# Mamba block with a mixture of experts: one state of each group from its own product, and two adds done by DMAs

## The chip, the cores and the metric

The kernel runs on one core of a Trainium2 chip. The metric is the device time of one execution in microseconds. A core has a matrix engine (TensorE, PE in the profile), a vector engine (DVE), a scalar engine (ACT), a general engine (POOL) and a synchronising engine (SP) that issues transfers here. Each runs its own list of instructions in order, and they wait for each other on semaphores.

## The reference

x is 8 sequences of 1024 tokens by 256 channels. It goes through a layer norm, a Mamba block and a residual add, then a layer norm, a mixture of experts and another residual add:

```
xp, z = in_proj(layernorm(x))                 # 2 x 512 channels
xc    = silu(causal_conv4(xp))
dt, B, C = x_proj(xc)                         # 64, 16, 16 columns
delta = softplus(dt_proj(dt) + dt_b)
h_n[t] = exp(delta * A_n) * h_n[t-1] + delta * xc * B_n[t]     # 16 states n for each of 512 channels
y     = sum_n h_n * C_n + D * xc
x     = x + out_proj(y * silu(z))
x     = x + square(relu(xn @ Ws1)) @ Ws2 + routed experts      # xn = layernorm(x)
```

The weights of the routed experts are cut to whole numbers, so a routed part is added only where a weight reaches 1. A flag decides at the end whether that path runs.

## The kernel before

The tokens are worked in NQ = 16 chunks of CH = 512 tokens. Channels are split into G = 4 groups of 128 partitions, and the 16 states of a group are worked in pairs. So a chunk has S = 32 steps (s = 0 to 31), eight for each group; step s of group g handles states 2(s % 8) and 2(s % 8) + 1. k = 32c + s counts steps over all chunks. Each engine's program is one hand-written loop over c and s; what an engine does in step s stands there as `if s == ...` (`tensor` L446, `scalar` L805, `vector` L1116, `gpsimd` L1326, `sync` L1435). A number such as ("yt", -1, 3) in the tables below means: group 3 of stage yt, of the chunk before.

The core of a step:
- ACT computes the decay factors da = exp(delta * A_n), five steps ahead (`act_exp`, L624, a pair for each step).
- PE computes BX, the input term of four states at once (`pe_bx`, L225): 16 products of 32 x 128 by 32 x 128, from uT (u = delta * xc, transposed) and bd (B spread on diagonals). BX takes four PSUM banks and exists once, so a fill for states 4p to 4p + 3 waits until the four scans of the fill before it are done. Fills stand at the end of odd steps.
- DVE runs one scan for each state (`dve_scan`, L964), from da and BX to hs.
- POOL multiplies hs by C (`pool_times_c`, L1261), and PE sums it into Y by transposing products (`pe_sum`, L257, for step k - 2).

Around it, in fixed steps, stands all other work of neighbouring chunks: the projections and convolution of chunks ahead (`pe_z`, `pe_xp`, `pe_dbc`, `pe_dt`, `pe_ut`; `dve_tap` is one tap of the convolution, `dve_delta` and `act_softplus` make delta), the gate and output projection of the chunk before (`dve_gate`, `pe_yt`, `pe_out`, stage "res"), and its experts (`pe_hidden`, `pe_htr`, `pe_shared`, stage "o"). `dve_residual` (L1068) adds x to "res" and `dve_shared` (L1109) adds "o", both in x1, which SP had loaded with x (`sp_xr`, L1418) and later writes out (`sp_out`, L1430).

Eight PSUM banks exist: four for BX, two for Y (shared with the convolution), and PA and PB for everything else. The tables BANK_A and BANK_B (L17, L20) give the order in which stages use PA and PB, by step. `bank_uses` numbers the uses; a PE product for use n waits until use n - 1 has been read out and released (`e.wait_ge(out, n)`), and the reader releases it by `.then_inc(out, 1)`. Which engine releases a stage is in the code of the reader: `act_z`, `act_yt`, `act_ut`, `act_trc` on ACT, `dve_delta`, `dve_residual`, `dve_shared`, `dve_top` on DVE.

The lines that order ACT around two of these releases:

```
if s == 16:                                   # L873
    act_softplus(e, c, 3)
...
if s == 30 and on(c + 1):                     # L901
    act_softplus(e, c + 1, 1)
    act_z(e, c + 1, 2)
```

## Time and profile before

| | us |
|---|---|
| median of 3 runs | 1560.38 |
| lowest, highest | 1560.03, 1560.77 |
| span of the profiled execution | 1559.1 |
| busy PE, DVE, POOL, ACT in the span | 1454.6, 1475.8, 1399.0, 1257.4 |

The profiled execution spans 1559.1 us from its first to its last instruction, 1.3 us below the median of the runs. The first scan starts at 34.5 us and the last ends at 1537, with 16 chunks between them. TensorE's granted clock is 0.999 of full speed. A profile's timeline has one line for each run of like instructions: start, duration, engine, source line, operation, output <- inputs, shapes and number of records; in brackets how long the engine was idle just before and who ended that.

### The profile page before, as it was taken

How to read it: one execution, taken by the hardware profiler on the slowest of the kernel's cores; microseconds unless marked ns; L12 is line 12 of the kernel's file. 1: busy time of each engine (PE TensorE's matmuls, PEld its weight loads, DVE VectorE, ACT ScalarE, POOL GpSimd, SP SyncE). 2: the span in 40 equal slices, each digit the busy share in tenths (PEclk: the TensorE clock that was granted, in tenths of full speed). 3: DMA queues.
4: the chain of work that ended last, by engine and by line, in shares of the span. 5: the costliest groups of instructions: out<-in, count | busy, mean ns of one | idle time of the engine just before them, and what ended most of it. 6: DMA issues, size and time to landing. Idle time of an engine off the chain costs nothing.

```text
span 1559.1 us, 39641 instructions
## 1 busy us (share of the span) xinstructions
PE 1454.6 (93%) x15324; PEld 1134.1 (73%) x15324; DVE 1475.8 (95%) x1775; ACT 1257.4 (81%) x2099; POOL 1399.0 (90%) x1199
## 2 busy tenths in 40 slices
PE   8889999999999999999999999999999999999988
PEld 5666777776777777777777777767777677777777
DVE  6999999999999999999999999999999999998886
ACT  7987887887888888887887888888888887788752
POOL 2899999999999999998999989999998999989994
PEclk9999999999999999999999999999999999999999
DMA  5103031040402305032040301304031040401301
GB/s 161 61 3 136 2 101 66 9 157 3 143 22 65 101 3 164 1 93 73 4 163 3 138 28 47 120 3 164 2 97 69 4 149 3 137 15 43 123 2 56
DMA packets 78512, 106.48 MB, mean 68 GB/s; under 512 B 42289, under 2 KB 67761, under 8 KB 70130
## 3 DMA queue, kind: packets, MB, share of 16 engines
q1 hardware_dynamic: 78322, 103.92, 20.8%
q8 instruction: 123, 2.02, 0.5%
q14 instruction: 67, 0.55, 0.1%
HBM read 86.10 MB, written 17.30 MB: 66 GB/s over the span
## 4 chain that ended last, share of the span: by engine, by line
DVE 32%; PE 20%; ACT 18%; issue 17%; POOL 10%; DMA 1%; SPq 1%; DVEq 1%; ACTq 0%; POOLq 0%
DVE hs L974 29%; PE BX L239 9%; ACT da L638 8%; POOL hs L1271 8%; PE Y L299 3%; PE Y L263 2%; ACT xc L705 1%; DMA cb<-c_scratch 1%; SPq L1406 1%; ACT xp L673 1%; DVE st L986 1%; DVE Y L1005 1%; PE PB L349 1%; ACT x2n L775 1%; POOL rstd L1304 1%
## 5 line engine op out<-in xcount | busy, mean ns | idle before, releaser
L1271 POOL TENSOR_TENSOR hs<-hs,cb 128x1024 f32<-128x1024 f32 x512 | 1210.2, 2364 | 76.3 <-DVE hs L974 55.3
L974 DVE TENSOR_TENSOR_SCAN hs<-da,BX 128x512 f32<-128x512 f32 x1024 | 1165.6, 1201 | 55.5 <-PE BX L239 46.5
L638 ACT ACTIVATE da<-delta,a_neg 128x511 f32<-128x511 f32 (+1 forms) x1024 | 663.6, 711 | 24.9 <-DVE hs L974 24.5
L263 PEld LDWEIGHTS Y<-ident,hs 128*128 128x128 f32 x4096 | 464.5, 141 | 97.3 <-issue 58.0
L263 PE MATMUL Y<-ident,hs 128*128 128x128 f32 x4096 | 510.1, 273 | 14.5 <-POOL hs L1271 14.4
L239 PE MATMUL BX<-bd,uT 32*128 32x128 f32 x8192 | 301.3, 284 | 77.9 <-DVE hs L974 73.8
L239 PEld LDWEIGHTS BX<-bd,uT 32*128 32x128 f32 x8192 | 252.5, 187 | 138.8 <-DVE hs L974 137.7
L299 PE MATMUL Y<-xnT,w_in 128*128 128x512 f32 x240 | 117.6, 613 | 0.7 <-ACT gate L691 0.7
L673 ACT ACTIVATE xp<-Y 128x512 f32<-128x512 f32 x60 | 35.9, 598 | 100.4 <-PE Y L299 99.9
L324 PE MATMUL PA<-w_in,xnT 128*128 128x512 f32 x240 | 114.5, 599 | 0.0
L1005 DVE SCALAR_TENSOR_TENSOR Y<-xp,w_conv,Y 128x512 f32<-128x512 f32 x120 | 88.9, 741 | 3.0 <-ACT Y L675 1.4
L1289 POOL TENSOR_TENSOR u<-delta,xc 128x512 f32<-128x512 f32 x63 | 80.4, 1277 | 5.1 <-issue 5.1
L1267 POOL COPY hlast<-hs 128x2 f32<-128x2 f32 x256 | 47.7, 186 | 38.5 <-DVE hs L974 36.8
L324 PEld LDWEIGHTS PA<-w_in,xnT 128*128 128x128 f32 x240 | 43.2, 190 | 44.9 <-issue 43.1
L741 ACT ACTIVATE u<-PB 128x512 f32<-128x512 f32 x63 | 37.5, 596 | 46.8 <-PE PB L349 45.1
L349 PE MATMUL PB<-dbc,w_dt 97*128 97x512 f32 x126 | 70.9, 645 | 0.9 <-DVE dbc L1136 0.9
L758 ACT ACTIVATE uT<-PB 128x512 f32<-128x512 f32 x48 | 28.7, 597 | 49.8 <-PE PB L357 49.8
L299 PEld LDWEIGHTS Y<-xnT,w_in 128*128 128x128 f32 x240 | 40.8, 190 | 36.5 <-issue 28.7
L333 PE MATMUL PA<-xc,w_x 128*96 128x512 f32 x128 | 61.6, 603 | 0.2 <-ACT xc L687 0.2
L376 PE MATMUL PB<-w_out,ygT 128*128 128x256 f32 x240 | 60.8, 386 | 0.9
L376 PE MATMUL PA<-w_out,ygT 128*128 128x256 f32 x240 | 60.8, 386 | 0.0
L1281 POOL TENSOR_TENSOR da<-first,hlast 128x2 f32<-128x2 f32 x256 | 51.1, 199 | 0.0
(194 smaller groups left out, 1517.5 us busy)
## 6 DMA issues: line engine op xcount, KB each, us to landing
cb<-c_scratch SPq DMA_DIRECT2D x64, 1024.0 KB, 4.8
x<-in_x SPq DMA_DIRECT2D x16, 512.0 KB, 4.3
x_scratch<-x2T SPq DMA_DIRECT2D x16, 512.0 KB, 6.8
xt<-in_x SPq DMA_DIRECT2D x15, 512.0 KB, 5.3
bd<-bt SPq DMA_DIRECT2D x480, 1.0 KB
out<-x SPq DMA_DIRECT2D x15, 512.0 KB, 3.2
w_in<-in_in_wT SPq DMA_DIRECT2D x1, 1024.0 KB, 8.4
c_scratch<-dbc SPq DMA_DIRECT2D x64, 8.0 KB, 1.5
```

The costliest lines, as they stand in the source:

```text
L239: mm = e.matmul(BX[:, q * CH + j * P:q * CH + (j + 1) * P], uT[rows, g, j, :], bd[rows, (NR * c + p) % BR, j, :, :].rearrange("p t n -> p ...
L263: mm = e.matmul(Y[(G * c + g) % 2][:, t * P:(t + 1) * P], hs[:, k % HR, q, t * P:(t + 1) * P], ident[:, :], is_transpose=True, start=False ...
L299: mm = e.matmul(bank[:, :], w_in[:, kk, g * P:(g + 1) * P], xnT[c % 2][:, kk, :], start=(kk == 0), stop=(kk == KD - 1))
L324: mm = e.matmul(bank[:, :], xnT[c % 2][:, kk, t * P:(t + 1) * P], w_in[:, kk, ED:2 * ED], start=(kk == 0), stop=(kk == KD - 1))
L333: mm = e.matmul(PA[0:FX, :], w_x[:, g, :], xc[:, (G * c + g) % XR, :], start=(g == 0), stop=(g == G - 1))
L349: e.matmul(bank[:, :], w_dt[:, g * P:(g + 1) * P], dbc[:, :].rearrange("f (j q t) -> f q j t", j=J, q=RT), start=True, stop=True).then_inc ...
L376: mm = e.matmul(bank[:, t2 * DM:(t2 + 1) * DM], ygT[:, g, t * P:(t + 1) * P], w_out[:, g, :], start=(g == 0), stop=(g == G - 1))
L638: e.activation(da[:, k % DR, q, h:], delta[:, g, h:], ACT.Exp, scale=a_neg[:, g, n:n + 1]).then_inc(s_da, 1)
L974: e.tensor_tensor_scan(hs[:, k % HR, q, :], da[:, k % DR, q, :], BX[:, :].rearrange("p (t n) -> p n t", n=RT)[:, n % RT, :], float(c % HV) ...
L1005: e.scalar_tensor_tensor(out=bank[:, :], in0=xp[:, g, kk:kk + CH], scalar=w_conv[:, g, kk:kk + 1], in1=bank[:, :], op0=ALU.mult, op1=ALU.a ...
L1271: e.tensor_tensor(hs[:, k % HR, :, :], hs[:, k % HR, :, :], cb[:, Q * p:Q * p + Q, :], ALU.mult).then_inc(s_hc, 1)
L1289: e.tensor_tensor(u[:, m % UR, :].rearrange("p (j q t) -> p q j t", j=J, q=RT), delta[:, g, :].rearrange("p (q j t) -> p q j t", j=J, q=RT ...
```

## The change

1. The last state of each group (15) no longer comes from BX. `pe_bu` computes its input term for 512 tokens by four products of uT (128 x 128) and b_diag, in which `act_diag` lays the 16th column of B on the diagonal (four small ACT operations a chunk). It is written to PA or PB at steps 7, 15, 23 and 31. The scan of that state reads that bank, and the refill of BX waits for 15 scans of a group instead of 16, so that it can run beside the 16th. The last BX fill of a group has 96 columns instead of 128 in each product.
2. `dve_residual` and `dve_shared` are gone. ACT copies "res" from its bank to x1, and "o" to x2n (`act_res`, `act_shared`). POOL issues a DMA that adds x from memory to x1 (`pool_add_x`, step 15), and one that adds x2n to the output in memory (`pool_add_shared`, step 3); SP writes x1 out at step 20 of the next chunk and loads no x into x1.
3. The orders are changed to fit: the bank tables, and the steps of several PE, ACT, DVE and POOL operations. bt has two buffers, and prob shares is_top's memory.

The diff, cut to its core:

```diff
@@ -14,12 +14,14 @@
 EXPS = "natural_log_exp_and_others"
 
 
-BANK_A = {0: [("z", 0, 3)], 2: [("o", -2, 1)], 4: [("yt", -1, 3)], 7: [("z", 1, 0)], 10: [("ut", 0, 2)], 11: [("res", -1, 1)],
-          12: [("trc0", 2, 0)], 16: [("z", 1, 1)], 18: [("dbc", 1, 0)], 22: [("bt", 1, 0)],
-          24: [("otr", -1, 0)], 25: [("otr", -1, 1)], 27: [("hl", -1, 1)], 30: [("z", 1, 2)]}
-BANK_B = {0: [("o", -2, 0)], 2: [("ut", 0, 1), ("trc", 2, 0)], 3: [("trc", 2, 1)], 4: [("yt", -1, 2)], 6: [("dt", 0, 2)],
-          8: [("res", -1, 0)], 13: [("trc0", 2, 1)], 15: [("yt", 0, 0)], 16: [("dt", 0, 3)], 20: [("ut", 0, 3)], 21: [("yt", 0, 1)], 24: [("dt", 1, 0)],
-          26: [("hl", -1, 0)], 28: [("ut", 1, 0)], 29: [("ht", -1, 0)], 30: [("dt", 1, 1), ("yt9", 0, 2)]}
+BANK_A = {0: [("z", 0, 3)], 1: [("o", -2, 0)], 2: [("dt", 0, 2)], 4: [("yt", -1, 3)], 6: [("trc", 2, 1)], 7: [("bu", 0, 0)],
+          10: [("ut", 0, 2)], 11: [("res", -1, 1)], 12: [("trc0", 2, 0)], 16: [("z", 1, 1)], 18: [("dbc", 1, 0)],
+          22: [("bt", 1, 0)], 23: [("bu", 0, 2)], 24: [("otr", -1, 0)], 25: [("otr", -1, 1)], 27: [("hl", -1, 1)],
+          30: [("z", 1, 2)], 31: [("bu", 0, 3)]}
+BANK_B = {2: [("o", -2, 1)], 3: [("yt", -1, 2)], 4: [("ut", 0, 1)], 5: [("trc", 2, 0)], 6: [("z", 1, 0)],
+          8: [("res", -1, 0)], 13: [("trc0", 2, 1)], 14: [("yt", 0, 0)], 15: [("bu", 0, 1)], 16: [("dt", 0, 3)],
+          20: [("ut", 0, 3)], 21: [("yt", 0, 1)], 24: [("dt", 1, 0)], 26: [("hl", -1, 0)], 28: [("ut", 1, 0)],
+          29: [("ht", -1, 0)], 30: [("dt", 1, 1), ("yt9", 0, 2)]}
 
...
@@ -225,7 +235,7 @@
         def pe_bx(e, m):
             c, i = divmod(m, QC)
             g, p = divmod(i, NR)
-            e.wait_ge(s_scan, RT * m)
+            e.wait_ge(s_scan, (N - 1) * (m // NR) + RT * p)
             if p == 0:
                 _, n, _, out = bank_of("ut", c, g)
                 e.wait_ge(out, n + 1)
@@ -233,13 +243,24 @@
                 e.wait_ge(s_bd, p + 1)
             if g == 0 and c:
                 e.wait_ge(s_bdd, 16 * KT * c)
+            ns = RT - 1 if p == NR - 1 else RT
             for j in range(J):
                 for q in range(RT):
                     rows = slice(q * KT, (q + 1) * KT)
-                    mm = e.matmul(BX[:, q * CH + j * P:q * CH + (j + 1) * P], uT[rows, g, j, :],
-                                  bd[rows, (NR * c + p) % BR, j, :, :].rearrange("p t n -> p (t n)"), start=True,
+                    mm = e.matmul(BX[:, q * CH + j * P:q * CH + (j + 1) * P].rearrange("p (t n) -> p t n", n=RT)[:, :, 0:ns],
+                                  uT[rows, g, j, :], bd[rows, (NR * c + p) % BR, j, :, 0:ns], start=True,
                                   stop=True, tile_position=(q * KT, 0))
             mm.then_inc(s_bx, 1)
+
+        def pe_bu(e, c, g):
+            bank, n, done, out = bank_of("bu", c, g)
+            e.wait_ge(out, n)
+            e.wait_ge(s_bdiag, c + 1)
+            e.wait_ge(*released("ut", c, g))
+            for j in range(J):
+                mm = e.matmul(bank[:, :].rearrange("p (q j t) -> p j q t", q=RT, j=J)[:, j, :, :], uT[:, g, j, :], b_diag[:, j, :],
+                              start=True, stop=True)
+            mm.then_inc(done, 1)
 
         def pe_skip(e, c, g):
             m = G * c + g
...
-                    if s == 2:
-                        pe_ut(e, c, 1)
-                    if s == 6:
-                        pe_dt(e, c, 2)
...
@@ -499,15 +516,16 @@
                         pe_xp(e, G * c + s // NP + 6)
                     if s == 0 and c:
                         pe_z(e, c, 3)
-                    if s in (0, 2) and on(c - 2):
-                        pe_shared(e, c - 2, s // 2)
-                    if s == 2 and c and on(c + 2):
-                        pe_trc(e, c + 2, 0)
+                    if s in (1, 2) and on(c - 2):
+                        pe_shared(e, c - 2, s - 1)
+                    if s == 2:
+                        pe_dt(e, c, 2)
                     if s in (12, 13) and c == 0:
                         pe_trc(e, 2, s - 12)
                     if on(c - 1):
+                        if s == 3:
+                            pe_yt(e, c - 1, 2)
                         if s == 4:
-                            pe_yt(e, c - 1, 2)
                             pe_yt(e, c - 1, 3)
...
+                    if s == 4:
+                        pe_ut(e, c, 1)
                     if on(c + 1):
-                        if s == 7:
+                        if s == 6:
                             pe_z(e, c + 1, 0)
...
@@ -532,6 +552,8 @@
                             pe_bt(e, c + 1)
                     if s == 24 and on(c + 1):
                         pe_dt(e, c + 1, 0)
+                    if s % NP == NP - 1:
+                        pe_bu(e, c, s // NP)
...
@@ -539,13 +561,13 @@
                     if s == 29 and on(c - 1):
                         pe_htr(e, c - 1)
                     if s == 30 and on(c + 1):
+                        pe_z(e, c + 1, 2)
                         pe_dt(e, c + 1, 1)
-                        pe_z(e, c + 1, 2)
                     if k >= 2:
                         pe_sum(e, k - 2)
-                    if s == 3 and c and on(c + 2):
-                        pe_trc(e, c + 2, 1)
-                    if s == 15:
+                    if s in (5, 6) and c and on(c + 2):
+                        pe_trc(e, c + 2, s - 5)
+                    if s == 14:
                         pe_yt(e, c, 0)
...
+        def act_diag(e, c):
+            if c:
+                e.wait_ge(*released("bt", c, 0))
+                e.wait_ge(*written("bu", c - 1, G - 1))
+            else:
+                e.wait_ge(s_b15, 1)
+                e.wait_ge(s_ident, 1)
+            for j in range(J):
+                ins = e.activation(b_diag[:, j, :], ident[:, :], ACT.Copy, scale=bt[c % 2][:, NR - 1, j, RT - 1:RT])
+            ins.then_inc(s_bdiag, 1)
...
+        def act_res(e, c, kk):
+            bank, n, done, out = bank_of("res", c, kk)
+            e.wait_ge(done, n + 1)
+            e.wait_ge(s_out, 16 * c)
+            e.activation(x1[:, 2 * kk:2 * kk + 2, :], bank[:, :].rearrange("p (t d) -> p t d", t=2), ACT.Copy).then_inc(out, 1)
+
+        def act_shared(e, c, kk):
+            bank, n, done, out = bank_of("o", c, kk)
+            e.wait_ge(done, n + 1)
+            e.activation(x2n[:, 2 * kk:2 * kk + 2, :], bank[:, :].rearrange("p (t d) -> p t d", t=2), ACT.Copy).then_inc(out, 1)
+
         def act_norm2(e, c):
             e.wait_ge(*shifted2(c))
-            for kk in range(2):
-                e.wait_ge(*released("res", c, kk))
-            if on(c - 1):
-                for kk in range(2):
-                    e.wait_ge(*written("o", c - 1, kk))
+            e.wait_ge(s_res, 16 * (c + 1))
+            e.wait_ge(s_acc, 16 * c)
             for t in range(TB):
                 ins = e.activation(x2n[:, t, :], x1[:, t, :], ACT.Identity, bias=shift2[:, t:t + 1],
                                    scale=rstd2[:, t:t + 1])
...
                         act_exp(e, 4)
                     if s == 1 and c:
                         act_z(e, c, 3)
+                    if s in (2, 3) and on(c - 2):
+                        act_shared(e, c - 2, s - 2)
                     if s == 2:
-                        act_ut(e, c, 1)
-                    if s in (3, 4) and c and on(c + 2):
-                        act_trc(e, c + 2, s - 3)
+                        act_softplus(e, c, 2)
+                    if s == 3 and on(c - 1):
+                        act_yt(e, c - 1, 2)
+                    if s in (5, 6) and c and on(c + 2):
+                        act_trc(e, c + 2, s - 5)
                     if s == 4 and c and on(c + 1):
                         act_xp(e, G * c + 6)
                     if s == 4 and on(c - 1):
-                        act_yt(e, c - 1, 2)
                         act_yt(e, c - 1, 3)
-                    if s == 6:
-                        act_softplus(e, c, 2)
+                    if s == 4:
+                        act_ut(e, c, 1)
                     if s == 10:
                         act_ut(e, c, 2)
+                    if s in (11, 15) and on(c - 1):
+                        act_res(e, c - 1, s // 4 - 2)
...
@@ -907,19 +955,22 @@
                         act_exp(e, k + DR - 1)
                     if s == 0 and c:
                         act_skip(e, c, 0)
-                    if s == 8:
-                        act_silu_z(e, c)
+                    if s == 5:
+                        act_diag(e, c)
                     if s in (12, 13) and c == 0:
                         act_trc(e, 2, s - 12)
                     if s == 7:
                         if on(c + 1):
                             act_z(e, c + 1, 0)
                         act_skip(e, c, 1)
+                    if s == 8:
+                        act_silu_z(e, c)
                     if s == 5 and c == 0:
                         act_norm(e, 2)
+                    if s == 14:
+                        act_yt(e, c, 0)
                     if s == 15:
                         act_skip(e, c, 2)
-                        act_yt(e, c, 0)
...
-        def dve_scan(e, k):
+        def dve_scan(e, k, q):
             c, i = divmod(k, S)
             g, p = divmod(i, NP)
-            e.wait_ge(s_bx, k // 2 + 1)
-            e.wait_ge(s_y, max(0, k - HR + 1))
-            if c % HV:
-                e.wait_ge(s_cr, S * (c // HV) + i + 1)
-            for q in range(Q):
-                n = Q * p + q
-                e.wait_ge(s_da, Q * k + q + 1)
+            if q == 0:
+                e.wait_ge(s_bx, k // 2 + 1)
+                e.wait_ge(s_y, max(0, k - HR + 1))
+                if c % HV:
+                    e.wait_ge(s_cr, S * (c // HV) + i + 1)
+            n = Q * p + q
+            e.wait_ge(s_da, Q * k + q + 1)
+            if n == N - 1:
+                bank, use, done, out = bank_of("bu", c, g)
+                e.wait_ge(done, use + 1)
+                e.tensor_tensor_scan(hs[:, k % HR, q, :], da[:, k % DR, q, :], bank[:, :],
+                                     float(c % HV), ALU.mult, ALU.add).then_inc(out, 1)
+            else:
                 e.tensor_tensor_scan(hs[:, k % HR, q, :], da[:, k % DR, q, :],
                                      BX[:, :].rearrange("p (t n) -> p n t", n=RT)[:, n % RT, :],
                                      float(c % HV), ALU.mult, ALU.add).then_inc(s_scan, 1)
...
+                    if s == 13 and on(c + 1):
+                        dve_tap(e, G * c + 7 if c else G + 3, 0)
+                        dve_tap(e, G * c + 7 if c else G + 3, 1)
+                    if s == 14 and on(c + 1):
+                        dve_tap(e, G * c + 7 if c else G + 3, 2)
...
+                    if s == 24 and on(c + 2):
+                        dve_tap(e, G * c + 8, 0)
+                    if s == 25:
+                        if on(c + 2):
+                            dve_tap(e, G * c + 8, 1)
+                        if on(c + 1):
+                            dve_delta(e, c + 1, 0)
+                        if on(c + 2):
+                            dve_tap(e, G * c + 8, 2)
...
+                    if s == 28 and on(c - 1):
+                        dve_top(e, c - 1, 1)
+                    if s == 29 and on(c + 2):
+                        dve_tap(e, G * c + 9, 0)
+                        dve_tap(e, G * c + 9, 1)
...
+        def pool_add_x(e, c):
+            for kk in range(2):
+                e.wait_ge(*released("res", c, kk))
+            e.dma_start(x1[:, :, :], x_v[c], accum_op=ALU.add).then_inc(s_res, 16)
+
+        def pool_add_shared(e, c):
+            for kk in range(2):
+                e.wait_ge(*released("o", c, kk))
+            e.wait_ge(s_out, 16 * (c + 1))
+            e.dma_start(out_v[c], x2n[:, :, :], accum_op=ALU.add).then_inc(s_acc, 16)
...
-                        if s == 7:
+                        if s == 1 and c:
+                            pool_u(e, c, 1)
+                        if s == 4:
                             pool_u(e, c, 2)
                         if s == 17:
                             pool_u(e, c, 3)
-                    if on(c + 1):
-                        if s == 25:
-                            pool_u(e, c + 1, 0)
-                        if s == 31:
-                            pool_u(e, c + 1, 1)
+                    if s == 3 and on(c - 2):
+                        pool_add_shared(e, c - 2)
+                    if s == 15 and on(c - 1):
+                        pool_add_x(e, c - 1)
+                    if s == 25 and on(c + 1):
+                        pool_u(e, c + 1, 0)
```

SP's `sp_x` moves from step 6 to 8, and `pe_fill`, which keeps PE busy in the last two chunks, stands in one step less. Before the loops, one small DVE copy is added for the first chunk's b_diag.

## Rows read from the trace of the kernel before

**Rows 1.** The page: busy time by engine; scans and their idle time ahead.
```profile
PE 1454.6 (93%) x15324; PEld 1134.1 (73%) x15324; DVE 1475.8 (95%) x1775; ACT 1257.4 (81%) x2099; POOL 1399.0 (90%) x1199
...
L974 DVE TENSOR_TENSOR_SCAN hs<-da,BX 128x512 f32<-128x512 f32 x1024 | 1165.6, 1201 | 55.5 <-PE BX L239 46.5
```
**Rows 2.** Busy time by engine in one chunk (span, PE, PEld, DVE, ACT, POOL).
```profile
786.10:879.99 93.89, 88.87 (x945) 69.09 (x945) 91.51 (x111) 78.27 (x132) 87.30 (x75) 1.00 0.22 72
```
**Rows 3.** Timeline of PE: start, duration (us), line, out<-in, records, idle before.
```profile
797.16 0.60 PE L273 MATMUL PB<-ident,xt 128*128 128x128 f32 x4
...
803.64 1.17 PE L239 MATMUL BX<-bd,uT 32*128 32x128 f32 x32
...
804.75 1.12 PE L349 MATMUL PB<-dbc,w_dt 97*128 97x512 f32 x2
...
805.71 1.04 PE L263 MATMUL Y<-ident,hs 128*128 128x128 f32 x8
...
806.59 1.88 PE L324 MATMUL PA<-w_in,xnT 128*128 128x512 f32 x4
...
809.54 1.17 PE L239 MATMUL BX<-bd,uT 32*128 32x128 f32 x32 [0.20 <-DVE hs L974]
...
828.19 2.00 PE L376 MATMUL PA<-w_out,ygT 128*128 128x256 f32 x8
...
850.53 1.17 PE L239 MATMUL BX<-bd,uT 32*128 32x128 f32 x32 [0.17 <-DVE hs L974]
...
853.46 0.50 PE L340 MATMUL PA<-ident,dbc 96*128 96x96 f32 x4
...
856.38 1.17 PE L239 MATMUL BX<-bd,uT 32*128 32x128 f32 x32 [0.68 <-DVE hs L974]
...
862.44 1.17 PE L239 MATMUL BX<-bd,uT 32*128 32x128 f32 x32
...
864.03 1.09 PE L396 MATMUL PB<-w_hr,x2T 128*128 128x136 f32 x8
```
**Rows 4.** Timeline of DVE, the same columns.
```profile
809.40 0.72 DVE L1009 SCALAR_TENSOR_TENSOR xc<-xp,w_conv,Y 128x512 f32<-128x512 f32 x1
...
810.04 0.68 DVE L1044 SCALAR_TENSOR_TENSOR delta<-PB,u 128x512 f32<-128x512 f32 x1
...
810.78 4.55 DVE L974 TENSOR_TENSOR_SCAN hs<-da,BX 128x512 f32<-128x512 f32 x4
...
821.68 0.68 DVE L1072 TENSOR_TENSOR x<-x,PB 128x512 f32<-128x512 f32 x1
...
874.64 0.24 DVE L1082 MAX8 top<-PA 128x8 f32<-128x8 f32 x2
...
874.91 0.17 DVE L1084 TENSOR_TENSOR is_top<-PA,top 128x16 f32<-128x16 f32 x1
```
**Rows 5.** Timeline of ACT, the same columns.
```profile
797.80 0.60 ACT L654 ACTIVATE xnT<-PB 128x512 f32<-128x512 f32 x1 [0.36 <-PE PB L273]
...
805.91 0.60 ACT L741 ACTIVATE u<-PB 128x512 f32<-128x512 f32 x1
...
807.74 2.55 ACT L638 ACTIVATE da<-delta,a_neg 128x512 f32<-128x512 f32 x4
...
810.19 0.58 ACT L699 ACTIVATE gate<-PA 128x512 f32<-128x512 f32 x1
...
878.23 0.58 ACT L699 ACTIVATE gate<-PA 128x512 f32<-128x512 f32 x1
...
885.30 0.57 ACT L699 ACTIVATE gate<-PA 128x512 f32<-128x512 f32 x1
```
**Rows 6.** The page: POOL's product; loads of x (KB, us to landing); SP's timeline.
```profile
L1271 POOL TENSOR_TENSOR hs<-hs,cb 128x1024 f32<-128x1024 f32 x512 | 1210.2, 2364 | 76.3 <-DVE hs L974 55.3
...
x<-in_x SPq DMA_DIRECT2D x16, 512.0 KB, 4.3
...
801.66 0.38 SPq L1423 DMA_DIRECT2D x<-in_x  x1
```

193 lines of the change are left out of this document (84 added, 109 removed).

## The prediction

> **What bounds the kernel now.** I read the busy times first. The page puts DVE at 95% of the span, PE at 93% and POOL at 90% [rows 1]. The stretch from 786.10 to 879.99 us is one whole chunk (from its first BX fill to the next chunk's): 93.89 us, with DVE 91.51, PE 88.87, POOL 87.30 and ACT 78.27 us busy [rows 2]. Three engines are nearly full, so shares alone don't say what a freed microsecond is worth; the order of work does.
>
> The timelines of PE and DVE show a loop of two steps, which I call a period (16 in a chunk; period p holds steps 2p and 2p+1). PE fills BX (1.10 us), DVE scans its four states (4.55 us), and only then may PE fill again. Next scans start 1.24 us after a fill starts (809.54 to 810.78), so the loop can't be shorter than about 5.85 us, as 850.53 to 856.38 shows (5.90 behind two taps, 803.64 to 809.54) [rows 3, 4]; 16 x 5.85 = 93.6 of the 93.89 us. DVE's other work (two short operations, about 1.35 us) stands in the 1.30 us in which it would wait for the fill; its recorded idle there is 46.5 us in the whole run [rows 1]. PE has 4.75 us in a period for all work that is not the fill, and mostly needs 4.3 to 4.6. So the bound is a loop, and **PE has under half a microsecond to spare in most periods**.
>
> **Prices.** A PE burst's duration contains some 0.17 us of tail that the next burst overlaps (1.04 us, next start 0.87 or 0.88 later). With it taken off: eight transposes of hs 0.87, dt 0.96, a z or xp product 1.72 (1.82 behind a fill), a product of 256 columns in eight records 1.83 behind a fill, a transposed tile of four records 0.43 [rows 3]. pe_bu has no row of its own. It is four float32 products of 128 columns, eight records; the nearest row is eight records of 136 columns, 1.09 less 0.17 = 0.92 us, so 0.87. Bounds: 0.43 (four records) and 1.83 (eight of 256 columns) [rows 3]. On ACT, dt's start to the softplus' start is 1.16 us, its three operations take 1.83 until the next begins, one step's pair of exps 1.23, a copy out of a bank 0.58; PE goes on at once when the copy ends. A transpose of x handed over takes 0.64 + 0.60 = 1.24 us until its bank is free [rows 3, 5].
>
> **What is taken off.** Four adds of 0.68 us a chunk leave DVE [rows 4]. The fourth scan of a group's last period no longer reads BX, so that period could be 5.85 - 1.14 = 4.71 us (a scan is issued every 1.14 us). By DVE alone, with its new order, a chunk is: eight periods of 5.85, two of 5.90 (two taps), three of 4.71 (p3, p11, p15), p7 with a tap between its scans 5.35, p12 7.10, p14 6.35, together 91.45 us.
>
> **DVE's own losses.** Step 24 gets a tap between scans (0.64), and step 25 three operations behind its scans: 4.47 + 0.64 + 1.99 = 7.10 us instead of 6.06 (fills 856.38 to 862.44) [rows 3]. In p14, a max and compare (0.43) now stand between scans, and two taps behind: 6.35 instead of 5.85. The two taps of step 23 were free inside a wait [rows 4].
>
> **PE's work in the group ends.** Each now has pe_bu. p11: 1.10 fill + 1.82 xp + 0.33 bt + 0.87 bu + 1.74 sums = 5.86 us. p3: 1.10 + 1.82 + 0.43 + 0.87 + 1.74 = 5.96. So PE, not the scans, ends these periods, and the 4.71 is not reached: the gain of hiding the refill is gone before any wait is counted. The fill itself shrinks from 128 to 96 columns; bounds 0 and 0.27 us (a quarter), I take 0.15, since shorter products of the same number of records save a little less than in proportion [rows 3].
>
> **The banks.** PE and ACT each run in order, and a product may enter PA or PB only when the use before it is released. Four handovers become waits, each followed from the fill's start F:
> - *p1.* pe_yt of group 2 follows pe_shared(1) in PB. Its release, act_shared(1), is at ACT's step 3, behind softplus(2), which waits for dt(2), issued in the same step 2. dt starts at F + 1.24 + 0.44 (skip) + 0.87 (shared) = 2.55; ACT starts at 3.71, ends the softplus at 5.54, the exps at 6.77, the copy at 7.37; then yt 0.43 and sum 0.87: 8.70 instead of 5.85, **+2.85 us**. Behind this wait on PE are the transposes and the next fill, and DVE waits for that.
> - *p15.* z(2) now goes ahead of dt(1) on PE, but ACT still does softplus(1) before it copies z(2), and pe_bu(3) needs z's bank. dt starts at 2.92, ACT at 4.08, ends softplus at 5.91, z at 6.49; bu and sum 1.74: 8.23 instead of 5.85, less what the shorter fill saves: **+2.3 us**.
> - *p0.* The z(3) copy ended 7.64 us after the z(2) copy began [rows 5], since exps and norm lie between. It now ends at F + 5.32, and pe_shared(0), which moved to step 1 in the same bank, would start at 3.79: 7.10 instead of 5.85, **+1.25 us** in chunks 2 to 13.
> - *p3 and p7.* pe_bu stands directly behind trc(1) or yt(0) in the same bank. The release is 1.24 us after the transposes start, where 0.43 was enough. p3: 3.79 + 1.26 + 0.87 + 0.87 = 6.79; p7: 3.75 + 2.96 = 6.71. Less 0.15: **+0.8 and +0.7 us**.
> p2 gains a transpose: 5.95, +0.1.
>
> **POOL, ACT, DMA.** POOL gets two DMA issues a chunk. No row shows one on this queue; the bounds are 0.38 us (an issue on SP) and 2.36 us (one of POOL's own products), and I take 1 us, nearer the issue [rows 6]. 87.30 + 2 stays below even the 91.45 us of DVE's own work, so it costs nothing. The Trainium skill, page DMA: Bandwidth & Descriptors (Latency and other measured facts), gives about 1 us for the first byte on GpSimd's path against 0.6 us; no row here shows it, and the sum would be the same by it. The load of x lands after 4.3 us [rows 6]; the adding DMA is issued about F8 + 4.2 and needed by stats2 at F8 + 12.2, so 8 us cover it. ACT gains four copies (2.3 us) and four small products (about 0.9), and has 15 us free; nothing beyond the orders above.
>
> **The sum.** Chunks 2 to 13: 2.85 + 2.3 + 1.25 + 0.8 + 0.7 + 0.1 + 1.05 + 0.5 - 0.15 = 9.4 us each, 113 us. Chunk 1 has no shared product (5.3), chunk 0 none and no transposes of x (2.5), chunk 14 no xp (4.7), chunk 15 only p1 and p7 against faster group ends (1.3). Together 127 us on the profiled execution's span of 1559.1; the median stands 1.3 us above the span. 1560.4 + 127 is **1687 us**.
>
> **The rivals.**
> *Faster.* The handovers do not bite, and PE's new products go into gaps. Then DVE's 91.45 us rules: 2.4 us less in each of 15.5 chunks, 1523 us. It needs PE's other work in a group end below 3.6 us; the rows add up to 4.6 to 4.9. It also needs ACT to release shared(1) before dt's softplus, against its order. The skill's page Perfetto Trace Analysis (Identifying the Most-Contended Engine) says that busy time of matmuls is no measure of headroom and weight loads are; those are busy 69 of 93.89 us [rows 2], which by that rule leaves room. In this trace PE's next burst starts where the last ends, whatever the loads show. Chance 5%.
> *Partly absorbed.* The waits overlap more than I add (bu is at its lower bound of 0.43 us in all four group ends, 1.76 us a chunk, and ACT has the z(3) copy done in time, 1.25 us): 6.4 us in each of the twelve chunks and 10 us for the other four, about 1647 us. Chance 14%.
> *The adding DMA is late.* If it takes 11 us instead of 8, stats2 at step 19 stands ahead of DVE's scans and 3 us a chunk come on top: 1687 + 15 x 3 = 1732 us. It decides from 8 us on. For it: adding means a read as well as a write of x1. Against it: SP's loads land in half of that. Chance 10%.
> *No change.* Gain and waits balance: 2%.
> My forecast has 69%, and by itself reaches from 1655 to 1715. The range, 1638 to 1725, takes in the absorbed case and leaves out most of the late DMA. Faster by over 0.2% (about what a measurement can tell here) 5%, within it 2%, slower 93%.
>
> **What would show it.** In the profile after: PE waits of about 3 us on ACT's copy of the shared product ahead of the gate transposes in step 3, and of some 1.7 us on the z copy ahead of pe_bu in step 31; fills 8.7, 8.2 and 6.7 us apart at p1, p15 and p3/p7; DVE's idle ahead of scans up from 46.5 to over 150 us; POOL and ACT with more idle time. The prediction is wrong if fills at the group ends stand 4.7 us apart, if a row of pe_bu's eight records is under 0.5 us, or if DVE's idle ends on the DMA.

## The result, and the profile after

The changed kernel takes **1734.69 us** (median of 4 runs, 1732.35 to 1735.69) against 1560.3 us before: a ratio of 1.1114, 95% interval 1.1098 to 1.113. The forecast was 1687 us with a range of 1638 to 1725. The direction and the places were right, the size was not: the loss is 171.4 us by the two spans (1730.5 less 1559.1) where 127 were predicted.

The page of the changed kernel, in the parts shown of before in [rows 1] (busy time by engine; the scans with their idle time and what ended it; the gate transposes of step 3; the adding DMA of x with its KB and its time to landing):

```profile
span 1730.5 us, 40837 instructions
PE 1537.1 (89%) x15824; PEld 1203.8 (70%) x15824; DVE 1449.5 (84%) x1718; ACT 1309.2 (76%) x2221; POOL 1438.8 (83%) x1228
L1031 DVE TENSOR_TENSOR_SCAN hs<-da,BX 128x512 f32<-128x512 f32 x960 | 1099.2, 1202 | 156.0 <-PE BX L250 153.8
L1028 DVE TENSOR_TENSOR_SCAN hs<-da,PA 128x512 f32<-128x512 f32 x48 | 58.5, 1218 | 75.4 <-ACT da L662 63.4
L386 PE MATMUL PB<-ident,gate 128*128 128x128 f32 x192 | 35.1, 313 | 39.8 <-ACT x2n L811 39.8
x<-in_x POOLq DMA_DIRECT2D x15, 512.0 KB, 5.9
```

No engine is at 90% any more. PE's work grew by 82.5 us, DVE's fell by 26.3, and the scans' idle time went from 55.5 [rows 1] to 156.0 us, plus 75.4 us ahead of the 48 scans of state 15 that read PA. So time is lost in waits. Where, the timeline of PE shows over one chunk (868.84 to 974.61 us, 105.77 against the 93.89 of [rows 2]); these are its steps 0 to 3, 7, 15, and 31:

```profile
868.84 1.17 PE L250 MATMUL BX<-bd,uT 32*128 32x128 f32 x32
...
873.94 1.13 PE L434 MATMUL PA<-w_s,x2n 128*128 128x256 f32 x4 [1.14 <-ACT gate L723]
...
875.87 1.17 PE L250 MATMUL BX<-bd,uT 32*128 32x128 f32 x32
...
879.20 1.04 PE L284 MATMUL Y<-ident,hs 128*128 128x128 f32 x8
883.07 1.12 PE L386 MATMUL PB<-ident,gate 128*128 128x128 f32 x4 [2.84 <-ACT x2n L811]
883.98 1.91 PE L284 MATMUL Y<-ident,hs 128*128 128x128 f32 x8
885.82 1.17 PE L250 MATMUL BX<-bd,uT 32*128 32x128 f32 x32
...
892.00 1.15 PE L250 MATMUL BX<-bd,uT 32*128 32x96 f32 x32
893.08 1.98 PE L345 MATMUL PB<-w_in,xnT 128*128 128x512 f32 x4
...
897.06 1.16 PE L261 MATMUL PA<-b_diag,uT 128*128 128x128 f32 x8 [0.69 <-ACT xnT L678]
898.06 1.04 PE L284 MATMUL Y<-ident,hs 128*128 128x128 f32 x8
899.02 1.17 PE L250 MATMUL BX<-bd,uT 32*128 32x128 f32 x32
...
921.64 1.16 PE L261 MATMUL PB<-b_diag,uT 128*128 128x128 f32 x8 [0.69 <-ACT ygT L800]
...
972.65 1.16 PE L261 MATMUL PA<-b_diag,uT 128*128 128x128 f32 x8 [1.62 <-ACT gate L723]
```

The four handovers are there, with waits of 1.14 us (period 0), 2.84 (1), 0.69 (3 and 7, one handover in the prediction) and 1.62 (15). What the prediction did not have is what comes after the longest: the four transposes and the eight sums, which it priced at 0.43 and 0.87 us until the next starts, take 0.91 (883.07 to 883.98) and 1.84 (to 885.82). The windows of one microsecond around them (columns: length, busy time of PE, PEld, DVE, ACT, POOL, then PE's granted clock, DMA share and GB/s) say why:

```profile
882.00:883.00 1.00, 0.00 (x0) 0.00 (x0) 0.84 (x2) 1.00 (x2) 0.92 (x3) 0.73 0.00 0
883.00:884.00 1.00, 0.93 (x5) 0.93 (x6) 0.00 (x0) 0.02 (x1) 1.00 (x1) 0.50 0.00 0
884.00:885.00 1.00, 1.00 (x6) 1.00 (x5) 0.00 (x0) 0.78 (x2) 1.00 (x2) 0.50 0.07 16
885.00:886.00 1.00, 1.00 (x9) 0.67 (x11) 0.00 (x0) 1.00 (x2) 0.98 (x1) 0.56 0.00 0
886.00:887.00 1.00, 1.00 (x33) 0.88 (x33) 0.00 (x0) 0.04 (x1) 0.00 (x0) 1.00 0.43 32
```

Toward the end of the idle stretch (880.23 to 883.07) the granted clock falls to 0.50, the lower level of 1.2 GHz, and comes back some 3 us later. Fill to fill, the periods of this chunk against the forecast (the other six stayed at 5.85):

| period | 0 | 1 | 2 | 3 | 7 | 11 | 12 | 13 | 14 | 15 |
|---|---|---|---|---|---|---|---|---|---|---|
| before | 5.85 | 5.85 | 5.85 | 5.90 | 5.90 | 5.85 | 6.06 | 5.85 | 5.85 | 5.85 |
| forecast | 7.10 | 8.70 | 5.95 | 6.64 | 6.56 | 5.71 | 7.10 | 5.85 | 6.35 | 8.1 |
| after | 7.03 | 9.95 | 6.18 | 7.02 | 7.03 | 5.97 | 6.60 | 6.26 | 6.24 | 8.38 |

### The profile page after: what moved, and what is told of

Its sections match the earlier page's. It is cut to its first block, busy times and chain, and to the rows that moved or that the text cites. A ratio compares the mean times of both kernels' runs of the same rounds, so it can differ in the third digit from the quotient of the medians.

```text
span 1730.5 us, 40837 instructions
## 1 busy us (share of the span) xinstructions
PE 1537.1 (89%) x15824; PEld 1203.8 (70%) x15824; DVE 1449.5 (84%) x1718; ACT 1309.2 (76%) x2221; POOL 1438.8 (83%) x1228
## 4 chain that ended last, share of the span: by engine, by line
PE 41%; DVE 23%; ACT 18%; issue 12%; POOL 4%; DMA 1%; DVEq 0%; SPq 0%; POOLq 0%; ACTq 0%
DVE hs L1031 20%; PE BX L250 12%; PE Y L284 8%; ACT da L662 7%; PE Y L320 3%; POOL hs L1320 3%; PE PA L345 2%; PE PA L261 2%; PE PA L397 2%; PE PB L345 2%; ACT u L778 1%; ACT xt L668 1%; ACT u L776 1%; PE PB L370 1%; PE PB L386 1%
## 5 line engine op out<-in xcount | busy, mean ns | idle before, releaser
L1031 DVE TENSOR_TENSOR_SCAN hs<-da,BX 128x512 f32<-128x512 f32 x960 | 1099.2, 1202 | 156.0 <-PE BX L250 153.8
L662 ACT ACTIVATE da<-delta,a_neg 128x511 f32<-128x511 f32 (+1 forms) x1024 | 666.0, 712 | 5.5 <-DVE hs L1031 4.9
L284 PEld LDWEIGHTS Y<-ident,hs 128*128 128x128 f32 x4096 | 477.1, 143 | 111.5 <-issue 63.1
L284 PE MATMUL Y<-ident,hs 128*128 128x128 f32 x4096 | 535.0, 277 | 18.9 <-POOL hs L1320 18.6
L1028 DVE TENSOR_TENSOR_SCAN hs<-da,PA 128x512 f32<-128x512 f32 x48 | 58.5, 1218 | 75.4 <-ACT da L662 63.4
L345 PE MATMUL PA<-w_in,xnT 128*128 128x512 f32 x180 | 87.7, 609 | 0.0
L261 PE MATMUL PA<-b_diag,uT 128*128 128x128 f32 x384 | 53.7, 283 | 33.2 <-ACT gate L723 24.3
L1330 POOL TENSOR_TENSOR da<-first,hlast 128x2 f32<-128x2 f32 x256 | 74.7, 292 | 0.0
L261 PEld LDWEIGHTS PA<-b_diag,uT 128*128 128x128 f32 x384 | 46.5, 191 | 40.1 <-ACT gate L723 27.9
L386 PE MATMUL PB<-ident,gate 128*128 128x128 f32 x192 | 35.1, 313 | 39.8 <-ACT x2n L811 39.8
L800 ACT ACTIVATE ygT<-PB 128x512 f32<-128x512 f32 x48 | 28.4, 591 | 54.4 <-PE PB L386 54.4
```

Source lines behind the costliest of these rows:

```text
L261: mm = e.matmul(bank[:, :].rearrange("p (q j t) -> p j q t", q=RT, j=J)[:, j, :, :], uT[:, g, j, :], b_diag[:, j, :], start=True, stop=True)
L284: mm = e.matmul(Y[(G * c + g) % 2][:, t * P:(t + 1) * P], hs[:, k % HR, q, t * P:(t + 1) * P], ident[:, :], is_transpose=True, start=False ...
L345: mm = e.matmul(bank[:, :], xnT[c % 2][:, kk, t * P:(t + 1) * P], w_in[:, kk, ED:2 * ED], start=(kk == 0), stop=(kk == KD - 1))
L662: e.activation(da[:, k % DR, q, h:], delta[:, g, h:], ACT.Exp, scale=a_neg[:, g, n:n + 1]).then_inc(s_da, 1)
L1031: e.tensor_tensor_scan(hs[:, k % HR, q, :], da[:, k % DR, q, :], BX[:, :].rearrange("p (t n) -> p n t", n=RT)[:, n % RT, :], float(c % HV) ...
L1330: e.tensor_tensor(da[:, k % DR, :, 0], first[:, g, Q * p:Q * p + Q], hlast[:, g, Q * p:Q * p + Q], ALU.mult).then_inc(s_cr, 1)
```

## The experiments

Each run is told by its edit, to the changed kernel unless said otherwise. Theory A is in each case the chain of orders as the prediction has it, with what the trace of after added.

**1. ScalarE copies the shared product ahead of the softplus.** The costliest wait, period 1, is laid to the place of one copy in ScalarE's order.

```diff
-                    if s in (2, 3) and on(c - 2):
-                        act_shared(e, c - 2, s - 2)
+                    if s == 2 and on(c - 2):
+                        act_shared(e, c - 2, 0)
+                        act_shared(e, c - 2, 1)
                     if s == 2:
                         act_softplus(e, c, 2)
```

> The changed kernel with one edit: ScalarE copies the second half of the shared product (step 2) ahead of the softplus of group 2 instead of behind it. Theory A (the wait of 2.84 us in period 1 is the place in ScalarE's order, and the half clock is its consequence): the copy ends some 0.1 us before dt(2), so period 1 goes from 9.95 to about 5.9 us, 4.05 us in each of 14 chunks: 57 us less, 1678 us, and the granted clock stays at 1.00 there. Theory B (the half clock has another cause and stays): only the 2.84 us of the wait go, 40 us less, 1695 us. Theory C (the time comes back in another wait, such as uT behind the gate transposes): under 15 us less.

Measured: **1678.75 us**, ratio 1.0763 (1.0745 to 1.0781). Period 1 is 5.85 us in every chunk, the transposes of gate stand right behind the sum, the mean clock is 0.998. From PE's timeline of this run:

```profile
855.35 1.04 PE L284 MATMUL Y<-ident,hs 128*128 128x128 f32 x8
856.22 0.60 PE L386 MATMUL PB<-ident,gate 128*128 128x128 f32 x4
856.66 1.04 PE L284 MATMUL Y<-ident,hs 128*128 128x128 f32 x8
```

`act_shared(0)` stood ahead of the softplus before too, so what moved is the second copy: one copy put ahead of the softplus and the exps behind it is worth 56 us, a third of the loss, as theory A had it to within 1 us. The rival in which only the 2.84 us go (1695) and the one in which the time comes back elsewhere fall. This run shows that wait and clock go together, not yet that the idle time causes the clock.

**2. The wait stays, but TensorE is kept busy in it.** A tile of zeros is transposed and added into Y, 24 times, so nothing in the results or in the order of the others changes.

```diff
                         if s == 3:
+                            if on(c - 2):
+                                pe_zero(e, c, 24)
                             pe_yt(e, c - 1, 2)
```

> The changed kernel with nothing moved; 24 transposes of a tile of zeros, added into Y (which leaves it as it is), stand on TensorE just ahead of the gate transposes of step 3, where it otherwise idles 2.84 us. They take 24 x 0.109 = 2.6 us. Theory A (TensorE's clock falls to its lower level because it idled): the granted clock stays 1.00, the four gate transposes take 0.43 and the eight of hs 0.87 until the next starts, period 1 goes from 9.95 to 8.66; 1.29 us in 13 chunks, 17 us less, 1718 us. Theory B (the slow stretch comes from something else, such as the bank being read by ScalarE or the DMAs of that moment): no gain or a small loss, 1735 us or up to 5 us more.

Measured: **1716.97 us**, ratio 1.0998 (1.098 to 1.1017), period 1 between 8.66 and 8.68 in all 14 chunks from 2 on, mean clock 0.997. PE's timeline of this run (20 of the 24 zero transposes have a record):

```profile
875.25 2.35 PE L296 MATMUL Y<-ident,zt 128*128 128x128 f32 x20
877.83 0.66 PE L396 MATMUL PB<-ident,gate 128*128 128x128 f32 x4 [0.23 <-ACT x2n L823]
878.32 1.04 PE L287 MATMUL Y<-ident,hs 128*128 128x128 f32 x8
879.28 1.17 PE L253 MATMUL BX<-bd,uT 32*128 32x128 f32 x32
```

The transposes of gate take 0.49 and the sums 0.96, so the lower clock had cost 1.30 us of the 2.75. ScalarE's reads and the DMAs are there as before, so those rivals fall: the 17.7 us are the idle engine's lower clock, by themselves. 8.66 us is also what the prediction's sum for period 1 gave (8.70). The clock still falls once in chunks 7 and 13 of the profiled execution, in period 13, where nothing was filled (7.81 and 7.71 us against 6.36 in the other odd chunks).

**3. A third of the filling.** Eight transposes of zeros instead of 24, which leaves 1.97 us idle.

> As the run with 24 transposes of zeros ahead of the gate transposes, but with 8 of them (0.87 us): TensorE still idles some 1.97 us there. Theory A (the idle of 2.84 us is at the edge: the one of 2.55 us in the run with z(2) first kept its clock, and so did that of 2.84 us in chunk 2): the clock is kept, period 1 is 8.66 us, 1717 us, as with 24. Theory B (the wait must be filled for the most part): the clock falls all the same, and the time is that of the changed kernel, 1735 us.

Measured: **1731.96 us**, ratio 1.1093 (1.1075 to 1.1112). Theory A is wrong: only chunks 4, 8 and 10 keep the clock (periods 1 and 2 together 14.85 us). The nine other chunks from 2 to 13 and the last two lose it, at a point that shifts from chunk to chunk, in some so late that it is mostly the fill and the products of period 2 that are hit; in each of the nine the two periods take 16.40 to 16.46 us together. PE's timeline and windows in chunk 9 of this run:

```profile
990.10 0.66 PE L396 MATMUL PB<-ident,gate 128*128 128x128 f32 x4 [1.97 <-ACT x2n L823]
990.60 1.30 PE L287 MATMUL Y<-ident,hs 128*128 128x128 f32 x8
991.82 2.09 PE L253 MATMUL BX<-bd,uT 32*128 32x128 f32 x32
```
```profile
990.00:991.00 1.00, 0.90 (x8) 0.90 (x9) 0.00 (x0) 0.25 (x2) 1.00 (x1) 1.00 0.00 0
991.00:992.00 1.00, 1.00 (x10) 0.67 (x10) 0.00 (x0) 1.00 (x3) 1.00 (x2) 0.61 0.00 0
992.00:993.00 1.00, 1.00 (x20) 1.00 (x24) 0.00 (x0) 0.81 (x2) 0.93 (x2) 0.50 0.00 0
```

Here PE has worked for 1.1 us again when its clock falls. So the length of the one idle stretch doesn't decide it: in the changed kernel 2.84 us kept the clock in chunk 2 (its period 1 is 8.66) and lost it in all later ones, and here 1.97 us lost it in nine chunks of twelve. The 2.55 us of run 4, of which the expectation says that they kept the clock, lost it in chunks 2, 6, 7 and 11. Theory B's 1735 us is near what was measured, but it too had every chunk alike. The Trainium skill, page TensorE: Matmul & The Clock Gate (Part 1: The HAM clock gate), says that the chip's observation of the engine runs freely and is not started by the kernel; that agrees with code that is the same in each chunk and is hit in some. What the runs show is the price: 1.3 to 1.6 us each time it falls in period 1.

**4. ScalarE copies z(2) first.** TensorE writes z(2) ahead of dt(1) since the change, while ScalarE still did softplus(1) first.

```diff
                     if s == 30 and on(c + 1):
-                        act_softplus(e, c + 1, 1)
                         act_z(e, c + 1, 2)
+                        act_softplus(e, c + 1, 1)
```

> The changed kernel with one edit: ScalarE copies z(2) ahead of the softplus of group 1 (step 30), as TensorE now writes it first. Theory A (ScalarE's chain from dt(1) through exps, norm, exps, skip to the z(3) copy runs on its own clock): the wait of 1.62 us ahead of pe_bu goes and period 15 falls from 8.38 to 6.6, but the z(3) copy ends only 0.48 us earlier, so period 0 grows from 7.03 to about 8.3; net 0.5 us in each of 14 chunks, about 1728 us. Theory B (the two waits are independent): 1.8 us in each of 15 chunks, 27 us less, 1708 us.

Measured: **1737.24 us**, ratio 1.1134 (1.1116 to 1.1153), no gain. The wait of 1.62 us ahead of pe_bu is gone and period 15 falls from 8.38 to 6.49, but period 0 rises from 7.03 to 8.44, in four chunks to between 9.75 and 9.94. PE's timeline, period 0:

```profile
872.83 1.04 PE L284 MATMUL Y<-ident,hs 128*128 128x128 f32 x8
876.42 1.13 PE L434 MATMUL PA<-w_s,x2n 128*128 128x256 f32 x4 [2.55 <-ACT gate L723]
```

The wait has moved: the copy of z(3) hangs on ScalarE's chain (softplus, two pairs of exps, a norm of 2 us, exps, skip), and that chain starts with dt(1), not with the fill. A fill that comes 1.9 us earlier waits 1.4 us more there. Two waits that stand in a row behind one chain are one wait. Most of the 9 us above the forecast are the clock again (0.98 on average): the four long periods 0, and 1.6 us instead of 1.3 behind the wait of period 1 in most chunks.

**5. Without pe_bu.** The products of uT and diag(B) and the writes of b_diag are left out, the fill has 128 columns throughout and state 15 is scanned from BX; banks, orders and the adding DMAs stay.

```diff
-                    if s % NP == NP - 1:
-                        pe_bu(e, c, s // NP)
...
-            ns = RT - 1 if p == NR - 1 else RT
+            ns = RT
```

> The changed kernel without its products of uT and diag(B): the fill has 128 columns again, state 15 is scanned from BX, no b_diag is written; all orders, banks and the adding DMAs stay. Theory A (the price of pe_bu is what it adds on TensorE and the handover ahead of it; period 0 and 15 are tied by ScalarE's chain to the z(3) copy): periods 3, 7 and 11 fall from 7.02, 7.03 and 5.97 to 5.85, which is 2.46 us in 15 chunks, 37 us less. Period 15 falls by 2.5 us but period 0 gives it back, and since TensorE then idles some 3.7 us there, its clock falls there too, 1.3 us in 14 chunks: 1716 us (1698 if the clock does not fall). Theory B (pe_bu's wait in period 15 is independent): another 2.5 x 15 us, 1660 us.

Measured: **1747.63 us**, ratio 1.1194 (1.1175 to 1.1213): slower than with the products, and 32 us above theory A. Period 15 is 5.89, and period 0 is 9.55 to 11.33 in chunks 2 to 13. The waits of PE in this run and the windows behind the first of them:

```profile
PE PA L434 <- ACT gate L720: 47.3, 14, 3.7
PE PB L386 <- ACT x2n L808: 39.8, 14, 2.8
PE PB L397 <- ACT gate L720: 12.8, 13, 1.0
```
```profile
882.00:883.00 1.00, 0.00 (x0) 0.00 (x0) 1.00 (x2) 1.00 (x2) 0.92 (x3) 1.00 0.00 0
883.00:884.00 1.00, 0.37 (x1) 0.37 (x2) 0.05 (x1) 1.00 (x3) 1.00 (x1) 0.53 0.53 188
884.00:885.00 1.00, 1.00 (x3) 0.80 (x3) 0.00 (x0) 0.81 (x2) 1.00 (x2) 0.50 0.99 418
```

PE waits 3.7 us in period 0 and its clock falls there too in nine of these twelve chunks (not in 3, 10 and 12); both were expected. What was not: period 4 grows from 5.85 to 6.69, since the residual's product now reaches PB 0.99 us before the z copy has left it (8.38 in the three chunks where the clock falls behind that wait), and period 7 falls only to 6.55, not 5.85, for the third tap now stands between the scans of steps 14 and 15. pe_bu's waits had covered both. So this run doesn't price pe_bu; it shows that what the trace puts ahead of it is in good part owed to orders that were changed with it, and comes up elsewhere when it is gone. Run 8 leaves it out once ScalarE's copies are moved.

**6. Three copies moved.** As 1 and 4 together, and ScalarE copies z(3) at step 0, ahead of a pair of exps, instead of at step 1.

> As the kernel with mended handovers, but with pe_bu back in its place ahead of the sum of hs; only ScalarE's three copies are moved. Theory A (pe_bu behind the sum takes TensorE's wait away and gives it to DVE's scan of state 15 and to GpSimd behind it, so the order is worth little): periods 3 and 7 rise again to 7.02, periods 4, 8 and 10 fall to 5.85, 0.3 to 0.9 us a chunk more: 1640 to 1655 us. Theory B (the order of pe_bu is worth its 1.7 us of waits in full): 1664 us.

Measured: **1645.59 us**, ratio 1.0543 (1.0527 to 1.056), 89 us less than the changed kernel by three copies moved in ScalarE's order, and inside the expected 1640 to 1655. Period 0 is 6.61, period 1 is 5.85, period 15 is 6.49; periods 3 and 7 stand at 7.02 and 7.03.

**7. The sum ahead of pe_bu as well.** This takes away the last two handovers.

```diff
-                    if s % NP == NP - 1:
-                        pe_bu(e, c, s // NP)
...
                     if k >= 2:
                         pe_sum(e, k - 2)
+                    if s % NP == NP - 1:
+                        pe_bu(e, c, s // NP)
```

> The changed kernel with its four handovers mended and nothing else: ScalarE copies both shared products ahead of the softplus of group 2, z(2) ahead of the softplus of group 1, z(3) ahead of the exps of step 0, and TensorE does the sum of hs ahead of pe_bu in steps 7, 15, 23 and 31. Theory A (what is left is TensorE's own work): periods 0 and 1 at 5.85, 2 at 6.18, 3 and 7 at 6.05, 11 at 5.97, 12 to 14 as they are (6.55, 6.31, 6.27), 15 at 6.4 and seven at 5.85, together 96.5 us a chunk against 105.8: 1602 us, still some 2.7% slower than before. Theory B (the handovers were all there was against the change, and its gain appears when they are gone): below 93.9 us a chunk, 1555 us or less.

Measured: **1640.22 us**, ratio 1.0507 (1.0491 to 1.0523). Between the theories and 38 us above A. The forecast of 96.5 us a chunk read only TensorE's bursts; a chunk takes 98.43 or 99.05. Period 3 is 6.14 or 6.55 and not 6.05, 4 is 6.37 or 5.97, 8 is 5.97, 10 is 6.60 in even chunks, period 0 is 6.61. The timelines of DVE and POOL in period 3 of an even chunk, and of PE in its period 10:

```profile
842.04 3.44 DVE L1032 TENSOR_TENSOR_SCAN hs<-da,BX 128x512 f32<-128x512 f32 x3 [0.16 <-PE BX L250]
847.55 1.22 DVE L1029 TENSOR_TENSOR_SCAN hs<-da,PA 128x512 f32<-128x512 f32 x1 [2.07 <-PE PA L261]
...
848.84 0.18 POOL L1317 COPY hlast<-hs 128x2 f32<-128x2 f32 x1 [0.86 <-DVE hs L1029]
...
888.16 1.09 PE L284 MATMUL Y<-ident,hs 128*128 128x128 f32 x8 [0.76 <-POOL hs L1321]
```

pe_bu behind the sum lets PE go on, but DVE's scan of state 15 now waits 2 us for it at each group's end. POOL, which multiplies that state, starts 0.86 us late, and in an even chunk it has little room to make up for it: PE waits for POOL in periods 3 and 10 (0.27, then 0.25 and 0.76 us). Period 7 is 6.16. With run 6 beside it, the order of pe_bu is worth 5.4 us in all and not the 1.7 us a chunk of its waits: most of the wait has only changed its owner.

**8. The same without pe_bu.** The edit of 5 on top of 6.

> As the kernel with mended handovers, but without the products of uT and diag(B): 128 columns in every fill, state 15 scanned from BX. Theory A (pe_bu costs TensorE time in the group ends and hides nothing): periods 3, 7, 11 and 15 at 5.85, or up to 0.7 more where the taps now stand in period 7; 95.5 us a chunk, 1586 us, some 16 us less than with pe_bu. Theory B (the scan of state 15 beside the refill is worth something once nothing waits): slower than with pe_bu.

Measured: **1633.65 us**, ratio 1.0472 (1.0456 to 1.0488). Leaving pe_bu out gains 6.6 us against run 7, less than the 16 expected, and 12 against run 6, where it stands ahead of the sum. Neither is pe_bu's own price, since waits come up here too: period 0 is 7.24 instead of 6.61, with PE waiting up to 1.4 us for the z(3) copy, period 4 is 6.70 and period 7 is 6.55, as in run 5. What stays is the more telling part: without it the kernel is still 73 us slower than before. That is banks, orders and the adding DMAs, of which run 9 prices DVE's order and run 11 the DMAs; the new bank tables were not run by themselves.

**9. DVE's order of before.** To run 6: the taps and the comparison of steps 23 to 31 go back to where they stood (in step 25 delta stays ahead of the tap).

```diff
-                    if s == 24 and on(c + 2):
+                    if s == 23 and on(c + 2):
                         dve_tap(e, G * c + 8, 0)
-                    if s == 25:
-                        if on(c + 2):
-                            dve_tap(e, G * c + 8, 1)
+                        dve_tap(e, G * c + 8, 1)
+                    if s == 25:
...
```

> As the kernel with ScalarE's three copies moved, and DVE's taps and comparison of steps 23 to 31 where they stood before the change. Theory A (period 12 to 14 are long by DVE's new order): period 13 and 14 fall from 6.3 to 5.9 and period 12 from 6.55 to 6.1 in odd chunks, in even ones it stays at 6.5 by GpSimd; 1.1 us in 14 chunks, 15 us less than with the three copies alone. Theory B (TensorE's own work sets them): no more than 3 us less.

Measured: **1630.68 us**, ratio 1.0449 (1.0433 to 1.0465), 14.9 us less than run 6, as theory A had it. By the periods it is 0.8 to 1.0 us a chunk, and some of the rest is the clock, which falls once more in run 6's profiled execution than in this one. Periods 13 and 14 are 5.85. Period 12 is still 6.60 in even chunks, behind POOL, and 6.47 in odd ones, where 6.1 was expected: there two taps stand behind a scan of state 15 that waited 0.61 us for pe_bu, and the fill waits 0.91 us for DVE. One chunk of this, the best version of the change (the columns of [rows 2]):

```profile
819.79:918.34 98.55, 93.02 (x977) 72.67 (x976) 89.78 (x107) 81.70 (x140) 90.25 (x77) 1.00 0.27 70
```

Against [rows 2] DVE has lost 1.73 us of work, PE has gained 4.15 and POOL 2.95. The chunk of before took 93.89 us; PE alone would now fill 93.0 of them. The 4.66 us that this chunk still takes more are periods 3 and 7 (2.27, most of it pe_bu and its handover), 0 (0.76), 15 (0.64), 12 (0.54), 2 (0.33) and 11 (0.12).

**10. The norm behind the z(3) copy.** To run 9: ScalarE normalises x after that copy, not before it.

> As the kernel with three copies moved and DVE's order restored, and ScalarE normalises x of two chunks on behind the z(3) copy instead of ahead of it. Theory A (period 0 is 6.6 because the norm of 2 us is ahead of that copy): period 0 falls to 6.0, 0.5 us in 13 chunks, 7 us less than without the move, about 1625 us; this is about what the change's arrangement can reach, 4% slower than before. Theory B (period 0 waits for something else, such as DVE's conv bank): no gain.

Measured: **1631.0 us**, ratio 1.0453 (1.0437 to 1.0469), no gain. Period 0 is 5.85, better than expected, and period 1 is 6.67 instead of 5.85. The time came back one period later, a form of the failure that none of the two theories named: in period 1 PE's stream stops for 0.60 us behind the fill in a gap that the profile books on nobody ("issue"), and the copy of the first shared product, late by the norm, holds dt for 0.17 more.

```profile
827.12 0.63 PE L274 MATMUL Y<-ident,xc 128*128 128x128 f32 x4 [0.60 <-issue]
...
828.78 1.12 PE L370 MATMUL PA<-dbc,w_dt 97*128 97x512 f32 x2 [0.17 <-ACT x2n L811]
```

In that gap ScalarE ends the scaling of xc that pe_skip reads (826.32 to 827.03), also behind the norm; that this is the release is read from the times, not shown by a wait.

**11. The adding DMAs alone, on the kernel before.** ScalarE copies the four products out, two DMAs on GpSimd's queue add x and the output, DVE's stats of the residual stand two steps later, and SP writes out at step 20 of the next chunk; banks and the orders of all else are of before.

```diff
-                        if s == 11:
-                            dve_residual(e, c - 1, 0)
...
+                    if s in (11, 15) and on(c - 1):
+                        act_res(e, c - 1, s // 4 - 2)
...
+                    if s == 3 and on(c - 2):
+                        pool_add_shared(e, c - 2)
+                    if s == 15 and on(c - 1):
+                        pool_add_x(e, c - 1)
```

> The kernel before with one part of the change: ScalarE copies the residual's and the shared expert's products out of their banks, two adding DMAs on GpSimd's queue add x and the output, the stats of the residual stand in steps 19 and 21; banks and every other order are those of before. Theory A (the adding DMAs are hidden and DVE's 2.7 us of adds lay in its waits for the fill): 93.9 us a chunk, 1560 us, between 1556 and 1566. Theory B (GpSimd's two issues of 1.3 us or ScalarE's four copies come on top somewhere): over 2 us in 14 chunks, 1590 us or more. Theory C (DVE's adds were on the path): under 1545 us.

Measured: **1564.24 us**, ratio 1.0021 (1.0012 to 1.003). Theory A: DVE is 2.2 us less busy in a chunk and nothing is won, since those adds lay in its waits for the fill. There is even a small loss, nearly all of it in period 12 of even chunks, 6.53 against 6.05, where PE waits for POOL (PE's timeline of this run):

```profile
860.39 1.09 PE L264 MATMUL Y<-ident,hs 128*128 128x128 f32 x8 [0.28 <-POOL hs L1263]
861.32 0.60 PE L387 MATMUL PA<-ident,x2n 128*128 128x128 f32 x4
862.97 1.09 PE L264 MATMUL Y<-ident,hs 128*128 128x128 f32 x8 [1.04 <-POOL hs L1263]
```

**12. The same with both DMAs left out.** x is not added to the residual, nor the shared product to the output; a bare signal takes their place.

> The kernel before with the adding DMAs' part alone, but both DMAs left out: x is not added to the residual and the shared expert's product not to the output, a bare signal on SyncE's queue stands in their place. Everything else is as in the run of that part alone, which took 1564.24 us. Theory A (its 3.3 us over the kernel before are GpSimd's two issues of 1.3 us, which make its products late at period 12 of even chunks): 1561 us, period 12 of even chunks 6.05 again. Theory B (they come from ScalarE's copies or from the DMAs' traffic in another way): 1564 us if the copies, and period 12 stays 6.53.

Measured: **1560.62 us**, ratio 1.0 (0.9991 to 1.0009), period 12 of even chunks 6.05 or 6.06 again. The copies on ScalarE cost nothing and the 3.6 us are the two DMAs. That it is their issue on POOL and not their traffic fits the place (POOL's chain) but was not told apart. The Trainium skill, page DMA: Bandwidth & Descriptors (SWDGE vs HWDGE vs iDMA), has accumulating DMAs on GpSimd's path only, so by that page their issue can't be moved to the idle SyncE; no run here tried it.

## Why the prediction was wrong in size

**What bounds the kernel** held. The loop of fill and scans with PE full beside it is what every run showed. Where PE has little to do in a group's end, the period is 4.71 (chunk 14 and 15, period 11), as read from DVE's side; in every group end of chunks 1 to 13 of the changed kernel it is 5.96 or more, and PE ends it.

**Period 1** is the step that failed. The chain to 8.70 was right (8.66 in chunk 2, and in every chunk of run 2), but what stands behind the wait was priced at 0.43 and 0.87 us, the durations of a running engine. A PE that idles 2.84 us comes back at half its clock in 13 of 14 chunks, and that costs 1.3 to 1.6 us each, 17.7 us by run 2. The prediction wrote "PE waits of about 3 us" among its signs and put their effect on the clock at nothing, without a reason. That the sum came to 8.70 is in part luck: the wait ends 7.20 us after the fill's start, not 7.37, and the two bursts behind it take 1.45 at the full clock, not 1.30.

**The terms that were mis-sized** make as much again, about 16 us in chunks 2 to 13 (1.3 us each). The fill of 96 columns takes 1.08 us until the next start against 1.10, so it saves 0.02 and not 0.15: a quarter fewer columns in the same 32 records hardly count. pe_bu takes 0.89 us where PE is running (945.27 to 946.16) but 1.00 behind a wait (897.06 to 898.06). A sum that stands directly ahead of a fill takes 0.96 until the fill starts (898.06 to 899.02), not 0.87. Periods 3 and 7 are 0.38 and 0.47 above the forecast, mostly by these three. Period 2 is 1.11 + 1.82 + 0.43 + 0.44 + 1.83 + 0.55 = 6.18 us of bursts without a gap, where 5.95 were counted. Period 12 was priced too high (7.10 against 6.60) and 13 was forgotten: DVE's third operation behind step 25 makes PE's skip wait 0.72 us. DVE's new order as a whole was forecast at 1.55 us a chunk; periods 12 to 14 of this chunk grew by 1.34, and run 9 gives back 0.8 to 1.0 a chunk by its periods. Period 12 of even chunks is not DVE's at all: PE waits 0.35 and 1.04 us for POOL there. The prediction's sum for DVE alone is off by a trifle too: its periods add up to 91.53, not 91.45.

**Period 15 and period 0** were priced as 2.3 and 1.25 and came as 2.53 and 1.18. Their sum is nearly right (3.71 against 3.55); that they are one wait, so that mending the first alone wins nothing (run 4), the prediction did not say.

**The ends.** Chunks 0 and 1 lost 2.9 us more than forecast, and the first fill starts 1.1 us later (34.40 against 33.31; it lies between 33.0 and 34.4 over the runs, whatever the edit). Chunk 14 lost 4.8 more and chunk 15 with the tail 5.8. In both last chunks period 11 is 4.7 but 12 is 8.32 and 7.21: the rstd of the residual stands in POOL's order there, and POOL's timeline of the changed kernel has no gap behind it while PE waits for its products, 0.94 and 1.04 us in chunk 14, 0.77 and 0.94 in chunk 15. That this is the cause is read from the timelines; no run tested it. With the clock (1.6 and 1.45 us, over periods 1 and 2) this is most of the 11 us; the rest wasn't followed up.

Together: 17.5 (clock, 3 of it in the last two chunks) + 16 (sizes) + 4 (start and chunks 0 and 1) + 3 + 4.5 (chunks 14 and 15, without the clock in them) is the 45 us between 127 and 171.4. No single term explains the miss: with the clock kept (run 2) the time is 1717 us, still 30 above the forecast of 1687.

**POOL, ACT, DMA.** An issue takes 1.3 us on POOL (1 was taken), in both bounds' middle:

```profile
L1378 POOL DMA_DIRECT2D x<-in_x x15 | 19.8, 1318 | 0.0
L1384 POOL DMA_DIRECT2D out<-x2n x14 | 19.0, 1359 | 0.0
```

"It costs nothing" was nearly right: 3.3 us against the runs of before beside it (run 11). The reason given, that POOL's busy time stays below DVE's, was weak: in an even chunk POOL's timeline (of the changed kernel) has no idle time from 924.2 to 969.2 us, and there each microsecond counts. The rival of the late adding DMA did not come: it lands after 5.9 us where 8 were there, and stats2 never waits for it. Its number, 1732, is near the measured one by chance. The faster rival fell with run 7: with all four handovers mended nothing is won. On the rule on weight loads of the Trainium skill, page Perfetto Trace Analysis (Identifying the Most-Contended Engine), the runs give the same answer as the rows: weight loads are busy 74 of 105.8 us, and 73 of 98.5 in the best version, and PE still ends the long periods.

**One line of the profile misleads.** Ahead of the scan of state 15 it names ScalarE's exps ("DVE hs L1028 <- ACT da L662", 63.4 us in all). DVE's timeline at the end of the chunk, beside pe_bu at 972.65 above, which ends at 973.81:

```profile
973.91 1.22 DVE L1028 TENSOR_TENSOR_SCAN hs<-da,PA 128x512 f32<-128x512 f32 x1 [2.96 <-ACT da L662]
```

The scan starts 0.10 us after pe_bu ends; the exps of that step had long been written.

## What to carry to other kernels

A product that moves work from a full engine to a nearly full one needs room on the second in the same period, and its bank's last reader must come ahead, in the reader's own order, of whatever waits for later work: here three copies in ScalarE's order were 89 of 174 us. Price a new wait on TensorE with what follows it at the lower clock too (1.3 to 1.6 us each time here, in most chunks but not in all), and don't count on a short filler to prevent it. When one wait is mended, look one period on, and one engine on, before counting the gain.

## What the runs showed of the hardware that was not expected

- TensorE's clock falls to 0.50 around idle stretches, and the same stretch in the same program does it in some chunks and not in others: 2.84 us in 13 chunks of 14 (the changed kernel), 1.97 us in 11 of 14 (run 3), 2.55 us in 4 of 12 (run 4), 3.66 us in 9 of 12 (run 5). It may fall after work has begun again, 1.1 us after in chunk 9 of run 3 and 1.3 us after in its chunk 2. Filling 2.6 of the 2.84 us kept it in all 14 (run 2).
- It fell behind short stretches too: in chunk 9 of run 6, where PE idles 0.51, 0.93 and 0.81 us between 1003.7 and 1008.6 us, the granted clock falls to 0.50 at 1008.9 and period 13 is 7.81 instead of 6.36. Runs 1 to 9 each lose it so in one to three chunks, in period 13 (1.3 to 1.5 us) or, without pe_bu, in period 4 (1.7 us).
- A fill of 32 records takes 1.08 us at 96 columns and 1.10 at 128.
- The first burst of TensorE behind a wait takes 0.05 to 0.1 us more until the next can start (pe_bu 1.00 against 0.89, transposes 0.49 against 0.44), and so does a burst directly ahead of a fill (a sum 0.96 against 0.87, transposes of x 0.55 against 0.44).
- An adding DMA of 512 KB lands after 5.9 us where the plain load of x takes 3.5 in the same kernel, and its issue holds GpSimd for 1.3 us.
